# Decoder layer: weights unpacked a tile slot later, last solves with GpSimd to themselves, root and means moved in four drain slots

## The reference

```python
x = layernorm(x + delta_attention(x))          # 8 heads of 128
x = layernorm(x + cross_attention(x, ctx, ids))
x = layernorm(x + ffn(x))                      # int weights, (w - 128) * scale
# delta_attention, for each head, over T = 2 * 64 steps:
state = state * exp(g_t)
corr  = k_t @ state
state = state + k_t * ((v_t - corr) * b_t)
o_t   = q_t @ state
# k, v, q: projection, causal convolution of 4 taps, silu; q and k normalised
# o * rsqrt(mean(o*o) + eps) * o_norm_w * silu(gate), then the output projection
# ffn: silu(h @ Wg) * (h @ Wu) @ Wd, Wg, Wu, Wd unpacked from integers
```

## Time and profile before

| what | us |
|---|---|
| median of 3 runs (lowest, highest) | 1208.03 (1207.48, 1210.53) |
| the profiled run | 1208.44 |
| its span, first to last instruction | 1206.6 |
| PE busy | 1123.1 (93%) |
| DVE busy | 812.0 (67%) |
| ACT busy | 703.2 (58%) |
| POOL busy | 512.2 (42%) |

### The profile page before, as it was taken

The page is one execution under the profiler, slowest core; times in us unless marked ns, Lnnn a source line. Parts: engine busy times, 40 slices in busy tenths (PEclk is TensorE's granted clock), DMA queues, the critical chain, the costliest instruction groups (busy, mean ns, idle before and its releaser), DMA issues.

```text
span 1206.6 us, 28712 instructions
## 1 busy us (share of the span) xinstructions
PE 1123.1 (93%) x11460; PEld 776.1 (64%) x11460; DVE 812.0 (67%) x1444; ACT 703.2 (58%) x1212; POOL 512.2 (42%) x719
## 2 busy tenths in 40 slices
PE   7788899999999999999998899859999999999997
PEld 2444455555555555555554556649989989989976
DVE  4887768868778679678766554756555666665552
ACT  3776567667676676676767666524454344444443
POOL 1659484684783873973966811200010000011000
PEclk9999899999999999999999899979999999999999
DMA  3123234545455464555645522341112221112100
GB/s 119 45 54 79 68 61 68 117 77 75 102 83 99 86 98 76 116 111 110 119 71 147 169 57 63 109 175 45 45 48 52 51 68 50 45 45 50 30 15 9
DMA packets 147268, 93.74 MB, mean 78 GB/s; under 512 B 80672, under 2 KB 130720, under 8 KB 146240
## 3 DMA queue, kind: packets, MB, share of 16 engines
q1 hardware_dynamic: 145984, 91.71, 34.5%
q10 hardware_dynamic: 1152, 0.21, 0.1%
HBM read 54.77 MB, written 14.55 MB: 57 GB/s over the span
## 4 chain that ended last, share of the span: by engine, by line
PE 65%; POOL 15%; DVE 9%; issue 6%; ACT 3%; SPq 1%; DMA 1%; ACTq 0%; POOLq 0%; DVEq 0%
PE proj L498 15%; PE out L1581 5%; POOL inverse L1286 5%; POOL rank_one L1283 5%; PE turned_v_chain L1581 5%; PE proj L1639 4%; PE turned_v_chain L1647 4%; PE proj L1520 4%; PE gram L513 4%; DVE conv L1080 3%; PE gram L1555 2%; PE turned_v_chain L504 2%; PE decays L529 1%; PE proj L1569 1%; DVE inverse L1127 1%
## 5 line engine op out<-in xcount | busy, mean ns | idle before, releaser
L1080 DVE SCALAR_TENSOR_TENSOR conv<-proj,kq_weights,conv 128x504 f32<-128x504 f32 (+2 forms) x261 | 189.8, 732 | 32.4 <-ACT conv L810 26.0
L498 PE MATMUL proj<-xT,vg_weights 128*128 128x512 f32 x384 | 192.0, 624 | 3.1 <-DVE conv L1080 1.8
L1880 POOL TENSOR_TENSOR rope<-rope_part,rope_part 128x512 f32<-128x512 f32 x32 | 40.1, 1272 | 337.4 <-DVE rope_part L1817 337.4
L1080 DVE SCALAR_TENSOR_TENSOR conv<-proj,vg_weights,conv 128x504 f32<-128x504 f32 (+2 forms) x192 | 140.7, 733 | 51.8 <-ACT conv L810 46.9
L498 PE MATMUL proj<-xT,kq_weights 128*128 128x512 f32 x348 | 167.4, 607 | 0.2 <-DVE conv L1080 0.2
L1286 POOL TENSOR_TENSOR inverse<-inverse,rank_one 128x30 f32<-128x30 f32 (+14 forms) x240 | 125.6, 523 | 18.8
L1283 POOL TENSOR_TENSOR rank_one<-inverse 128x30 f32<-128x30 f32 (+14 forms) x240 | 117.0, 488 | 14.4
L498 PEld LDWEIGHTS proj<-xT,vg_weights 128*128 128x128 f32 x384 | 69.2, 194 | 67.9 <-issue 61.1
L498 PEld LDWEIGHTS proj<-xT,kq_weights 128*128 128x128 f32 x348 | 62.6, 190 | 74.6 <-issue 70.5
L1656 ACT ACTIVATE rstd<-rstd 128x1 f32<-128x1 f32 x48 | 9.7, 202 | 143.2 <-DVE rstd L1764 143.2
L810 ACT ACTIVATE conv<-proj,kq_weights 128x512 f32<-128x512 f32 x87 | 59.6, 687 | 56.8 <-PE proj L498 56.5
(11 more groups left out here) (254 smaller groups left out, 2472.0 us busy)
## 6 DMA issues: line engine op xcount, KB each, us to landing
kq_weights<-in_kq_w SPq DMA_DIRECT2D x32, 390.0 KB, 6.6
vg_weights<-in_vg_w SPq DMA_DIRECT2D x32, 390.0 KB, 6.2
o_scratch<-oT SPq DMA_DIRECT2D x32, 256.0 KB, 2.2
o_in<-o_scratch SPq DMA_DIRECT2D x16, 512.0 KB, 4.0
o_rs<-o_rs_quarters SPq DMA_DIRECT2D x88, 64.0 KB, 6.1
diagonal<-gram_decayed SPq DMA_DIRECT2D x128, 32.0 KB, 1.9
inverse<-inverse SPq DMA_DIRECT2D x32, 128.0 KB, 2.8
q_first<-rope SPq DMA_DIRECT2D x128, 32.0 KB, 1.9
```

The source lines that it names most:

```text
L498: mm = e.matmul(bank(c, u)[:], w[:, (k * 3 + c % 3) * 128:(k * 3 + c % 3 + 1) * 128], xT[g][:, k, :], start=(k == 0), stop=(k == KD - 1))
L1080: e.scalar_tensor_tensor(acc(c, u)[:, :, back:], src[:, :, 0:S - back], weights(c, u)[:, j:j + 1], acc(c, u)[:, :, back:], ALU.mult, ALU.a ...
```

## The change

- CUTS: from batch 1 on, cut 2 has one pair less, and cut 3 has pairs 25 to 30 and the scaling of the columns at its first place, ahead of W_scaled.
- `quiet(s)` holds for slots 33 to 36. There TensorE takes the means behind both turnings of v, after a wait for both V copies; `turn_v(0, ud)` waits for one root less. ScalarE does the table load for Ln, the root and `k_norms` behind the W copies. The scaling of oT by o_rs moves from GpSimd to VectorE (`scale_output`), ahead of `add_q_squares`.
- Slot 33: GpSimd scales the rows and does pairs 1 to 4 ahead of W_scaled; VectorE takes the norms of the last solve right behind its load, ahead of the convolution V0.
- Tile phase: the unpacking moves from the end of slot 2 to slot 3, behind `softmax_max(2)` and ahead of `hidden(0, 0)`.

```diff
@@ -128,7 +128,7 @@
 SOLVE = 13
 LOADED, NORMS, READY, K_NORM, TURNED, TURNED2 = 2, 3, 10, 11, 12, 13
 ELIM = 2 * (RB - 2) + 3
-CUTS = (((1, 1), (1, 1), (1, 5)), ((5, 10), (10, 14), (14, 16)), ((16, 20), (20, 23), (23, 26)), ((26, 30), (30, 31), (31, 31)))
+CUTS = (((1, 1), (1, 1), (1, 5)), ((5, 10), (10, 14), (14, 16)), ((16, 19), (19, 22), (22, 25)), ((25, 31), (31, 31), (31, 31)))
 FIRST_CUTS = ((1, 8), (8, 15), (15, 22), (22, 26), (26, 31))
 
 
@@ -275,6 +275,7 @@
         out_slots = {last_slot - 3: 0, last_slot - 1: 1}
         rope_slots = {last_slot - 2: 0, last_slot: 1}
         joined = lambda u: u + LAG < last_slot - 3
+        quiet = lambda s: U < s <= last_slot - 4
         low_later = lambda u: joined(u + 1)
         high_chain = EB[:].rearrange("p (b s) -> p b s", b=GB)
         acc = lambda c, u: conv[place[c, u] % 4]
@@ -693,7 +694,7 @@
 
                 for s in range(LAG + 1, SLOTS):
                     ua, ub, uc, ud = s, s - 1, s - LAG, s - LAG - 1
-                    if s > U and not low_later(ud - 1):
+                    if s > U and not low_later(ud - 1) and not quiet(s):
                         norm(ud - 1)
                     if live(uc):
                         chain_y(uc)
@@ -703,7 +704,7 @@
                         e.wait_ge(d_wc[uc % 2], 16 * (uc // 2 + 1))
                         e.wait_ge(s_silu[G], uc)
                         project(V0, uc)
-                    if s > U and low_later(ud - 1):
+                    if s > U and low_later(ud - 1) and not quiet(s):
                         norm(ud - 1)
                     if s == last_slot + 1:
                         ahead["out"](2)
@@ -711,7 +712,7 @@
                         chain_inverse_low(uc)
                     if live(ud):
                         e.wait_ge(s_silu[V1], ud + 1)
-                        wait(e, s_ln, ud)
+                        wait(e, s_ln, ud - 1 if quiet(s) else ud)
                         turn_v(0, ud)
                     if live(uc):
                         if live(ub):
@@ -728,6 +729,9 @@
                     if live(ud):
                         e.wait_ge(s_v, 2 * ud + 1)
                         turn_v(1, ud)
+                    if quiet(s):
+                        e.wait_ge(s_v, 2 * ud + 2)
+                        norm(ud - 1)
                     if s in rope_slots:
                         ahead["turn_x1"](rope_slots[s])
                     if s == last_slot:
@@ -938,13 +942,14 @@
                 for s in range(LAG + 1, SLOTS):
                     ua, ub, uc, ud, uo = s, s - 1, s - LAG, s - LAG - 1, s - LAG - 2
                     h, late_q = solve_at(s, 6), live(s - 1)
-                    if live(ub) or live(uo):
+                    if (live(ub) or live(uo)) and not quiet(s):
                         e.preload_act_table_set(LN_EXP)
                     if late_q:
                         tap(Q, ub)
                     elif live(uc):
                         tap(V0, uc)
-                    if live(uo):
+
+                    def root():
                         e.wait_ge(s_norm, uo + 1)
                         if by_rows(uo):
                             wait(e, d_rs, 64 * uo)
@@ -953,16 +958,18 @@
                             e.wait_ge(s_gr, uo)
                             o_ln, o_mean = o_rs[:], VB
                         e.activation(o_ln, o_mean, ACT.Ln, scale=float(2 ** O_SHIFT), bias=guard[:, 0:1]).then_inc(s_ln, 1)
-                    if live(uo):
                         e.wait_ge(s_ln, uo + 1)
                         e.activation(o_ln, o_ln, ACT.Exp, scale=-0.5).then_inc(s_rs, 1)
+
+                    if live(uo) and not quiet(s):
+                        root()
                     if s in rope_slots:
                         ahead["rsqrt"](0, rope_slots[s])
                     if s == last_slot + 1:
                         ahead["exp"](0)
                     if live(ub):
                         exp_between(ub)
-                    if h is not None:
+                    if h is not None and not quiet(s):
                         k_norms(h)
                     if live(uc) and late_q:
                         tap(V0, uc)
@@ -982,6 +989,11 @@
                         copy_w_high(uc)
                         if low_later(ud):
                             copy_w_low(ud)
+                    if quiet(s):
+                        e.preload_act_table_set(LN_EXP)
+                        root()
+                        if h is not None:
+                            k_norms(h)
                     if s in rope_slots:
                         ahead["copy_x1"](rope_slots[s])
                     if live(uc):
@@ -1145,6 +1157,11 @@
                     e.wait_ge(s_osq, u + 1)
                     e.wait_ge(s_qsq, u + 1)
                     e.tensor_tensor(o_sum[:], o_sum[:], flat(q_sq[u % (LAG + 1)]), ALU.add).then_inc(s_osum, 1)
+
+                def scale_output(u):
+                    e.wait_ge(s_rs, u + 1)
+                    e.wait_ge(s_og, u + 1)
+                    e.tensor_tensor(oT[u % 2][:], oT[u % 2][:], o_rs[:], ALU.mult).then_inc(s_gr, 1)
 
                 def less_sum(u):
                     m = M[u % LAG][0:64, :, 32:]
@@ -1213,10 +1230,10 @@
                     if last_batch:
                         solve_load(loading, 0)
                         solve_load(loading, 1)
+                        solve_norms(loading)
                     if live(uc):
                         convolve(V0, uc)
                     if last_batch:
-                        solve_norms(loading)
                         gate_output()
                     if live(uo) and not last_batch:
                         gate_output()
@@ -1241,6 +1258,8 @@
                     if s >= LAG and live(ua):
                         conv_step(K1, ua, 2)
                         conv_step(K1, ua, 3)
+                    if quiet(s):
+                        scale_output(uo)
                     if live(ud) and s > U:
                         add_q_squares(ud)
                     if loading is not None and not last_batch:
@@ -1365,7 +1384,12 @@
                             eliminate(0, FIRST_CUTS[4])
                             scale_columns()
                     elif solving:
+                        if cut == 0 and s > U:
+                            scale_rows()
+                            eliminate(h, CUTS[cut][2])
                         eliminate(h, CUTS[cut][0])
+                        if cut == 3:
+                            scale_columns()
                     if live(ud):
                         e.wait_ge(s_wloout, ud + 1)
                         e.wait_ge(s_solve, SOLVE * batch(ud) + K_NORM)
@@ -1376,9 +1400,7 @@
                                         ALU.mult).then_inc(s_wk, 1)
                     if solving and h > 0:
                         eliminate(h, CUTS[cut][1])
-                        if cut == 3:
-                            scale_columns()
-                    if live(uo):
+                    if live(uo) and not quiet(s):
                         e.wait_ge(s_og, uo + 1)
                         if by_rows(uo):
                             e.wait_ge(d_rs, 64 * (uo + 1))
@@ -1389,7 +1411,7 @@
                         e.wait_ge(s_osq, ud + 1)
                         e.wait_ge(s_qsq, ud + 1)
                         e.tensor_tensor(o_sum[:], o_sum[:], flat(q_sq[ud % (LAG + 1)]), ALU.add).then_inc(s_osum, 1)
-                    if solving and h > 0:
+                    if solving and h > 0 and not (cut == 0 and s > U):
                         if cut == 0:
                             scale_rows()
                         eliminate(h, CUTS[cut][2])
@@ -1847,6 +1869,10 @@
                         if live(u2):
                             mask_scores(u2)
                             softmax_max(u2)
+                        if u4 == 0:
+                            dequantize("w_gate")
+                            dequantize("w_up")
+                            dequantize("w_down")
                         if live(u4):
                             hidden(0, u4)
                             hidden(1, u4)
@@ -1857,10 +1883,6 @@
                             hidden(3, u4)
                         if live(u2):
                             softmax_sum(u2)
-                        if s == AHEAD:
-                            dequantize("w_gate")
-                            dequantize("w_up")
-                            dequantize("w_down")
                         if u3 == 0:
                             e.wait_ge(done["scaled"], U)
                         if live(u3):
```

## The result

The kernel before took 1208.24 us (median of 8 runs, 1203.16 to 1210.53), the changed kernel 1216.22 (8 runs, 1214.52 to 1220.36). The medians differ by 8.0 us, where 8.6 were forecast. The ratio, which weighs all runs, is 1.0081 with an interval from 1.0060 to 1.0102; that is 9.8 us (7.2 to 12.3), and the forecast lies inside it. The profiled run of the changed kernel took 1216.13; its span is 1214.3 against 1206.6.

What follows compares the result with a forecast made beforehand. TensorE, busy 93% of the span, was taken as the bound, with only its waits to win. Drain +5.8 and unpacking +2.8 gave +8.6 on the median 1208.03: 1216.6 us, range 1211.5 to 1220.

Steps and rivals of the forecast that it cites:

- The sum and its shares: Whole kernel: +5.8 us for the drain and +2.8 for the unpacking, together +8.6; chance 0.52.
- the drain: Slots 33 to 36: chain of unit 28 starts 4.3 us later, plus 1.5 of slow clock; +5.8 (2 to 9).
- the unpacking: Tile slots 2 and 3: wait only moves (+0.1), 2.7 us of slow clock behind 10.7 idle; +2.8 (-0.5 to +3.6).
- The cuts, slots 12 to 32: Later W_scaled loses nothing in slots 12 to 28; slot 32 gains 2.0 us, of which slot 33 leaves nothing.
- The ring: Slots 34 to 36: V0 waits for the gate's silu behind ScalarE's copies, root and table loads; 15.4 us a turn.
- The clock term: TensorE idling before V0 of units 26 and 27 brings one slow stretch, 1.5 us at unit 28 (0 to 3.0).
- GpSimd's solve: Last solve, batch 7: starts 6.5 us earlier but ends at 687.2 instead of 688.69.
- (B): Slots 34 to 36: relief of GpSimd decides, ring of 13.4 us or less, unit 28 1.9 earlier; 1208.9, chance 0.19.
- (C): Tile slot 2: much of the 12 us is kept as the unpacking ends earlier; with (B) 1203, chance 0.12.
- (D): Only one part costs, the drain or the unpacking; 1212 to 1213, chance 0.14.
- (E): ScalarE: four table loads cost more than their rows show, 1220.6 with one us each; chance 0.03.

Runs made afterwards that it cites:

- e2: Changed kernel with the unpacking put back to its old place in tile slot 2; ratio 1.0052 to the kernel before.
- e1: Kernel before with only the unpacking moved to tile slot 3, behind softmax_max(2); ratio 1.0033.
- e12: Changed kernel with 90 extra transposes in TensorE's wait for the unpacked weights; turning of x2 to nope product took 7.16 us (changed kernel 8.63).
- e9: Kernel before with only means behind the turnings and root and k_norms behind the W copies, slots 33 to 36; ratio 1.0099.
- e10: Kernel before with only the scaling of oT moved from GpSimd to VectorE, ahead of add_q_squares, slots 33 to 36; ratio 0.9976.
- e5: Kernel before with the unpacking behind normalize(1,0) in tile slot 2; ratio 0.9993.
- e6: Kernel before with e5's unpacking place, e10's scaling, and the last solve turned ahead of add_q_squares; 1201.29 us, ratio 0.9951.

## Why the prediction was right, step by step

**The sum and its shares.** Forecast +8.6 = 5.8 + 2.8; the medians give +8.0, the ratio 9.8. By the ratios of e2 and e1 the shares are 6.3 (4.0 to 8.6) and 4.0 (1.6 to 6.3). From profile to profile they are 8.05 and 1.3, with 1.6 given back at the end, but that sets the slow clock stretches of one execution against those of another. The total was right and both shares lie inside these intervals. That the sum came so close in the profile (7.7 for 8.6) is in part luck: the drain was 2.25 too low, the unpacking 1.5 too high, and the 1.6 at the end had no term.

**The cuts, slots 12 to 32.** Nothing was lost there: the chain of unit 23 comes 0.46 later than before, of which 0.14 was there at the first chain. From the chain of unit 23 to that of unit 24 the changed kernel takes 14.78 for 16.77, and all seven profiles with the new cuts gain 1.99 to 2.03 there: the forecast 2.0. At unit 24 itself it is 1.5, because of the 0.46. Slot 34 starts at 644.84, forecast 644.4, with the output product waiting 1.27 for W_scaled as said.

**The ring.** The mechanism was right at every joint: the gate's silu is last at V0 of units 26 and 27 (forecast waits 3.3 and 2.7, found 1.81 and 2.54; the first is smaller as TensorE itself came there at 660.2, 2.2 later than counted), GpSimd waits before W_scaled, add_q_squares stands ahead of the turning. V0 of unit 26 started at 662.02, forecast 661.3; from there to V0 of unit 27 it took 17.55, forecast 15.4, and 1.8 of the 2.15 between them is the slow V0.

**The clock term, mis-sized.** I took one slow stretch of 1.5 for two idlings. Both brought one: V0 took 3.75 and 2.45 for 1.98, 1.77 and 0.47, and V1 of the second 2.11 for 1.88, in all 2.5. That is 1.0 of the 2.25 by which the drain was under-counted. Another 0.9 was there before the ring closed: slot 34 began 0.44 late (the 0.46 of unit 23) and the W copies of unit 25 came at 655.79 instead of 654.9. There the gate's silu held V0 of unit 25 for 0.46, and VectorE's copy of Y held TensorE for 0.38 behind an o_sum that took 1.00 instead of 0.69. The remaining 0.4 is the ring itself, 15.8 instead of 15.4.

**GpSimd's solve, off by 3.9.** I had it end at 687.2; it ended at 691.05, later than before, above all because W_scaled of slot 35 ran at 673.86, after 3.74 of waiting for a copy of W, where I had 670.9. It decided nothing: the square on ScalarE came 5 us later still.

**The unpacking.** The out product of tile 3, the late rows, the mask, the unpacking behind it: as forecast, down to a wait of 10.69 (forecast 10.7) and +0.1 against -0.2. The clock term behind that wait was mis-sized: 2.7 by the row after 9.77 of idling, 1.5 found, and e12 shows that it is clock. The other 2 of the 3.4 I could not see: the old place took 129.2 in the one profile I had and takes 127.2 on average, so that more was given up than I counted.

**The rivals.** (B), relief of GpSimd, is refuted by e9: root and means alone cost 12.6 us with GpSimd's queue as before. The side of it that holds is e10, the scaling alone, 0.24% faster. (C) fell because the mask did wait for the late rows; its idea, an earlier unpacking that TensorE hardly sees, is what e5 and e6 do. (D) fell with e1 and e2, which both cost; its own sums give 1212.8 to 1213.8, not 1212 to 1213. (E) fell: the loads at 690.45 and 693.12 start within 0.02 of the operation before them and are followed as fast. The Trainium skill (ScalarE: Activation LUTs, What ACT_TABLE_LOAD costs) gives 1.28 us for the load, which the trace confirms, and a drain of 1.38 more, which none of these rows shows.

## What to carry to other kernels

An operation with a table of its own that is moved from the idle head of a slot to a place behind the last copies takes its two loads into the path of everything queued behind it; here 3.9 us a slot outweighed the small waits it removed. When one engine is the gapless one, take work off it (e10), but test each edit alone: of the four edits here one helps, one can't be told from nothing, as its gain and its loss cancel, and two cost. A long one-off job like an unpacking isn't helped by being merely later: so late that TensorE stood waiting for its result it cost (e1). Right behind the last operand that TensorE needed it did not (e5), though that wasn't told from the old place either.

## What the runs showed of the hardware

**Slow stretches that the code doesn't decide.** Behind the same idle time TensorE's products sometimes ran at half clock and sometimes not, with 1.7 us between the two. From 248 to 250 us the granted clock was 1.00 in the profile of before and 0.50 in that of e1. TensorE around the chain of unit 6, where the code of the two kernels is the same, before and then e1:

```profile
246.16 0.42 PE L688 MATMUL turned_v_chain<-o_sum,ones_mean 128*32 128x128 f32 x8 [1.52 <-POOL o_sum L1391]
...
247.14 1.12 PE L529 MATMUL decays<-steps,between_lhs 128*128 128x512 f32 x2
248.10 1.88 PE L498 MATMUL proj<-xT,vg_weights 128*128 128x512 f32 x4
```
```profile
246.57 0.43 PE L688 MATMUL turned_v_chain<-o_sum,ones_mean 128*32 128x128 f32 x8 [1.47 <-POOL o_sum L1391]
...
247.55 1.98 PE L529 MATMUL decays<-steps,between_lhs 128*128 128x512 f32 x2
249.33 2.77 PE L498 MATMUL proj<-xT,vg_weights 128*128 128x512 f32 x4
```

Of the thirteen changed versions eight have a step of 1.7 between the chains of units 6 and 7, others of the same size follow at units 11, 15 and 19 (there back), and up to unit 23 little else sets their profiles apart. What the first step goes with is the time of arrival: the eight started the first product shown at 246.32 to 247.45, the six without it (before among them) at 245.63 to 246.44. Why that should matter stays open. At the chain of unit 23 two profiles lie up to 4.5 us apart, 3.4 of it by these steps, so a stretch has to be compared from a common point.

**VectorE and GpSimd slow each other.** In e10 the o_sum of slot 36, started at 685.02 beside GpSimd's column scaling (684.40 to 686.75), took 2.28 instead of 0.69; before, the same operation took 1.84. It ended 0.55 behind the scaling in both, and again in e1 and e5 (0.56 and 0.55), wherever it had started: it waited and then ran. GpSimd's next operation, begun while the sum still ran, was longer in its turn, 1.72 for 1.28 before and 1.50 for 1.04 in e10. The rows agree with the Trainium skill (SBUF — State Buffer, SBUF: two separate sides), by which the two engines share a pair of ports that one of them holds for a whole instruction. VectorE in e10, then VectorE and GpSimd before:

```profile
685.02 2.28 DVE L1148 TENSOR_TENSOR o_sum<-o_sum,q_sq 128x512 f32<-128x512 f32 x1 [1.33 <-ACT o_sum L1013]
```
```profile
687.40 1.84 DVE L1147 TENSOR_TENSOR o_sum<-o_sum,q_sq 128x512 f32<-128x512 f32 x1 [1.98 <-ACT o_sum L1012]
```
```profile
688.65 1.72 POOL L1387 TENSOR_TENSOR oT<-oT,o_rs 128x512 f32<-128x512 f32 x1
```
